# A graph layer and a mixture of experts in one kernel: the self-loop by VectorE, counts behind the last unit, and another order of the power, the routing and the fills

## The chip, the cores and the metric

The kernel runs on one core of a Trainium2 chip. The metric is the device time of the whole program in microseconds; lower is better. The engines are TensorE (PE), VectorE (DVE), ScalarE (ACT), GpSimd (POOL) and SyncE (SP), which only issues DMAs here.

## The reference

2048 tokens of 256 features and a 2048 x 2048 adjacency of zeros and ones:

```python
deg = jnp.maximum((adj != 0).astype(jnp.float32).sum(-1), 1.0)
# gnn: a_hat = adj + eye; a_norm = dinv * a_hat * dinv; pooled = a_norm @ x + x; relu(pooled @ W + b)
x = x + _L0_gnn_ref(_layernorm(x), adj, deg[..., None], W, b)
# ffn: gate, top 1 of 8 experts, softmax of one = 1; silu/gate/down per expert; plus gelu(xf @ sw1.T) @ sw2.T
x = x + _L0_ffn_ref(_layernorm(x)[None], gate_w, w1, w2, w3, sw1, sw2)[0]
```

(The kernel scales both sides by one inverse degree per row.) The eye in `a_hat` is the self-loop: each token's own row of z = norm(x) @ W is added to its neighbours' sum.

## The kernel before, in words

All matmuls are float32 split into a high half (fp32r) and a low half (the rest), and run as several fp32r products. For every operand some engine copies the high half (mostly ACT) and another subtracts it to get the low half (mostly POOL, with `tensor_tensor` from SBUF).

*Stages.* The first quarter computes z for 16 tiles of 128 tokens and adds up neighbours for output tiles 0 to 3. `agg_quarter(q)` for q = 1, 2, 3 does the same for four more output tiles each: 16 input tiles j, each with eight matmuls (L1304, L1306) that need `a_hi` (ACT, L667) and `a_lo` (POOL, L477) of that tile. Then `agg_end` (L1310 to L1315) adds the self-loop by four matmuls of `ident_r` with z. `gate` and `degrees` follow; `degrees` needs the neighbour counts of DVE (L922, L925). Then comes, for q = 1 and 2, a shared stretch of 16 units m (`shared`): `shared_up(m)` (L1405), gelu and `gel_hi` on ACT (L726, L730), `gel_lo` on POOL (L490), and two units later `shared_down` (L1427, L1429), which waits for `gel_lo`. Behind the fourth quarter the stretch has 32 units (LAST to LAST + 31), of which DVE makes the last `gel_lo`s (from LAST + DVE_AT on). In between, PE does gate, rank and transpose work for the routing. At last come 23 steps of expert work (`up`, `hid_transposes`, `down`), one for each block of 128 sorted rows.

*Order.* Every engine's order is written out by hand; semaphores tie them. Within the shared stretches POOL and ACT also make the first eight tiles' halves of the next quarter (`LEAD` = 8), one between two pairs of units. POOL makes `exp_of_z` (a power, L548) there behind the fourth of these. The other eight tiles' halves follow in the quarter itself, each when PE has freed its slot. The adjacency comes in chunks of two tiles in four buffers `araw`; the load of chunk n (L380) waits until chunk n - 4 is counted and split. POOL issues the `scatter` of sorted rows (L554): four behind the low halves of a quarter for an earlier quarter, and eight more among the last units.

*SP's order at the end.* It issues the expert chunks n = 0, 1, ... (L417; 12 an expert, four buffers), each waiting for the low half (`elo_ok`) of n - 3. Ahead of n = 8 it writes eight fill rows (L409), behind n = 11 it waits for all scatters, for the routing table (`routed`) and for the fills, and loads the first three blocks of sorted rows (L425), one behind each of n = 11, 12, 13. DVE makes the low halves of expert chunks 0 to 7 (`low_chunk`, L1155), POOL those from 8 on (L520).

*What the change touches on DVE.* `first_products` (L999) and `finish_gnn` (L1006, L1010) turn the neighbour sums into the new x, in the order `low * dinv2 + (z + bias)`, then `agg * dinv2 + low`, then relu and residual. `add_bias` (L916) makes z + bias in place. The loop from L1101 has the counts, statistics and `scales` of each quarter.

## Time and profile before

| | us |
|---|---|
| median of 3 runs (lowest, highest) | 475.96 (475.58, 478.83) |
| profiled execution, its own time | 476.37 |
| its span | 474.6 |
| PE busy | 445.6 (94%) |
| POOL busy | 322.6 (68%) |
| DVE busy | 255.2 (54%) |
| ACT busy | 208.4 (44%) |
| chain that ended last: PE, POOL, DVE, ACT | 72%, 11%, 6%, 4% |

All times below are from the start of the span. A row of a timeline has the start, the length, the engine (with q: its queue of instructions, mostly DMA issues), the line, what is written and read, the number of instructions merged, and in brackets the idle time before it and who ended that. An instruction that waits for a shared resource after its start is listed with that time in its length.

### The profile page before, as it was taken

Reading aid. Unit: us, or ns where it says so; the run is one execution under the profiler, and the core shown is the slowest. Engines: PE = TensorE matmul, PEld = TensorE weight load, DVE = VectorE, ACT = ScalarE, POOL = GpSimd, SP = SyncE. Lnnn points to the kernel's source line nnn. Section 1 sums busy time; section 2 is a strip of 40 time slices with the busy share of each in tenths; the row PEclk is TensorE's granted clock in tenths of the full one; section 3 lists DMA queues with packets and bytes.
Section 4 is the critical chain, followed back from the end, with each engine's and each line's share of the span. In section 5 each row is a group of like instructions: output and inputs, shape, how many; then the busy total and the mean of one; then the engine's idle time right before and its main releaser. Section 6 shows DMA issues by size and latency. Waiting matters only on the chain.

```text
span 474.6 us, 8852 instructions
## 1 busy us (share of the span) xinstructions
PE 445.6 (94%) x2635; PEld 381.7 (80%) x2636; DVE 255.2 (54%) x540; ACT 208.4 (44%) x462; POOL 322.6 (68%) x296
## 2 busy tenths in 40 slices
PE   7889999989999899999898999999999999999992
PEld 6779777878888788888787888888888888888872
DVE  5884979663767455888934433343334334433430
ACT  4777596655456354645442323232323222322330
POOL 3548975897488765779875498885677579883112
PEclk9999999999999899999999999999999999999997
DMA  8555534130440407685665999997898552663000
GB/s 272 205 176 182 159 107 136 55 110 24 134 135 1 134 2 254 228 310 207 195 200 151 377 353 378 339 341 240 305 330 303 184 203 36 75 79 44 2 0 0
DMA packets 39612, 82.61 MB, mean 174 GB/s; under 512 B 5024, under 2 KB 14752, under 8 KB 37536
## 3 DMA queue, kind: packets, MB, share of 16 engines
q1 hardware_dynamic: 27024, 47.60, 30.8%
q0 software_dynamic: 7536, 29.39, 20.2%
q10 hardware_dynamic: 5024, 5.27, 3.6%
q8 instruction: 15, 0.25, 0.2%
q14 instruction: 13, 0.11, 0.1%
HBM read 74.74 MB, written 8.41 MB: 175 GB/s over the span
## 4 chain that ended last, share of the span: by engine, by line
PE 72%; POOL 11%; DVE 6%; ACT 4%; issue 3%; DMA 2%; SPq 1%; POOLq 0%; ACTq 0%; DVEq 0%
PE bank L1486 26%; PE bank L1513 9%; PE bank L1304 9%; PE bank L1514 5%; PE bank L1306 4%; PE bank L1499 4%; POOL gel_lo L490 4%; PE bank L1405 4%; PE bank L1427 3%; PE bank L1262 2%; POOL a_lo L477 2%; POOL ering L520 2%; PE bank L1429 1%; PE bank L1288 1%; POOL sorted_x L554 1%
## 5 line engine op out<-in xcount | busy, mean ns | idle before, releaser
L1486 PE MATMUL bank<-ering,xsT_hi 128*128 x368 | 121.7, 402 | 1.4 <-POOL ering L520 1.4
L477 POOL TENSOR_TENSOR a_lo<-araw,a_hi 128x512 fp32r<-128x512 f32 x48 | 69.9, 1467 | 28.4 <-ACT a_hi L667 27.8
L1220 DVE SCALAR_TENSOR_TENSOR hid<-bank,xs,sil 128x512 f32<-128x512 f32 x46 | 34.5, 751 | 93.9 <-ACT sil L803 93.9
L1486 PEld LDWEIGHTS bank<-ering,xsT_hi 128*128 128x128 f32 x368 | 69.4, 189 | 17.8 <-issue 1.9
L1486 PE MATMUL bank<-ering,xsT_lo 128*128 x184 | 73.0, 396 | 0.0
L1304 PE MATMUL bank<-zz,a_hi 128*128 128x512 f32 x192 | 69.9, 404 | 2.4 <-POOL a_lo L477 2.4
L803 ACT ACTIVATE sil<-bank 128x512 f32<-128x512 f32 x46 | 27.5, 598 | 101.4 <-PE bank L1486 101.4
L520 POOL TENSOR_TENSOR ering<-eraw,ering 128x512 fp32r<-128x512 f32 x40 | 51.4, 1303 | 29.2 <-DMA ering<-in_experts 20.3
L1513 PE MATMUL bank<-ering,hidT_hi 128*128 x184 | 67.5, 407 | 1.2 <-DVE hidT_lo L1228 1.2
L520 POOL TENSOR_TENSOR ering<-eraw_more,ering 128x512 fp32r<-128x512 f32 x48 | 60.6, 1292 | 8.3 <-PE bank L1262 5.1
L625 POOL DMA_INDIRECT out<-y_rows,row_token x23 | 35.8, 1554 | 36.8 <-DVE y_rows L1236 31.4
L1427 PE MATMUL bank<-sw_r,gel_hi 128*128 128x512 f32 x128 | 50.4, 415 | 8.7 <-POOL gel_lo L490 6.9
L1306 PE MATMUL bank<-zz,a_lo 128*128 128x256 f32 x192 | 53.8, 280 | 0.0
L490 POOL TENSOR_TENSOR gel_lo<-gel,gel_hi 128x256 fp32r<-128x256 f32 x56 | 43.2, 778 | 14.9 <-ACT gel_hi L730 14.3
L1514 PE MATMUL bank<-ering,hidT_lo 128*128 x184 | 51.7, 281 | 0.0
L1304 PEld LDWEIGHTS bank<-zz,a_hi 128*128 128x128 f32 x192 | 36.1, 188 | 11.6 <-POOL a_lo L477 2.8
L1513 PEld LDWEIGHTS bank<-ering,hidT_hi 128*128 128x128 f32 x184 | 34.6, 188 | 8.7 <-issue 1.4
L925 DVE SCALAR_TENSOR_TENSOR count<-araw,count 128x1024 bf16<-128x1024 f32 x28 | 40.0, 1428 | 1.6
L1486 PEld LDWEIGHTS bank<-ering,xsT_lo 128*128 128x128 f32 x184 | 34.8, 189 | 7.3
L1405 PE MATMUL bank<-xfT_hi,sw_hi 128*128 128x256 f32 x128 | 37.3, 292 | 0.0
L1427 PEld LDWEIGHTS bank<-sw_r,gel_hi 128*128 128x128 f32 x128 | 24.7, 193 | 15.1 <-POOL gel_lo L490 6.7
L730 ACT ACTIVATE gel_hi<-gel 128x256 fp32r<-128x256 f32 x64 | 26.8, 418 | 22.5 <-PE bank L1429 22.2
(165 smaller groups left out, 931.1 us busy)
## 6 DMA issues: line engine op xcount, KB each, us to landing
araw<-in_adj_t SPq DMA_DIRECT2D x32, 512.0 KB, 4.5
eraw<-in_experts SPq DMA_DIRECT2D x48, 256.0 KB, 4.7
ering<-in_experts POOLq DMA_DIRECT2D x8, 1536.0 KB, 9.3
eraw_more<-in_experts SPq DMA_DIRECT2D x48, 256.0 KB, 5.9
ering<-in_experts POOLq DMA_DIRECT2D x8, 1024.0 KB, 7.1
ering<-in_experts POOLq DMA_DIRECT2D x8, 512.0 KB, 5.2
xs<-sorted_x ACTq DMA_DIRECT2D x20, 129.0 KB, 3.7
sw_raw<-in_sw_t ACTq DMA_DIRECT2D x2, 1024.0 KB, 7.5
```

Of the source, the lines that this page charges most:

```text
L477: pool.tensor_tensor(lo_part(s), araw[:, u // CJ, u % CJ, :], hi_part(s).bitcast(F32), ALU.subtract).then_inc(adj_lo_ok, 1)
L490: pool.tensor_tensor(gel_lo[:, u, :], gel[:, u, :], gel_hi[:, u, :].bitcast(F32), ALU.subtract).then_inc(sh_lo, 1)
L520: pool.tensor_tensor(ering[:, slot, 1, c * ECW:(c + 1) * ECW], raw, ering[:, slot, 0, c * ECW:(c + 1) * ECW].bitcast(F32), ALU.subtract).t ...
L625: pool.indirect_dma_start(out=out, out_offset=bass.IndirectOffsetOnAxis(ap=row_token[:, s:s + 1], axis=0), in_=y_rows[:, s, :], in_offset= ...
L925: dve.scalar_tensor_tensor(into, araw[:, r, :, :], 0.0, into, ALU.not_equal, ALU.add).then_inc(adj_counted, CJ)
L1304: pe.matmul(acc(q, it)[:, :], hi_part(s)[:, it * P:(it + 1) * P], zt, start=first, stop=False)
L1306: ins = pe.matmul(acc(q, it)[:, 0:D], lo_part(s)[:, it * P:(it + 1) * P], zt[:, 0:D], start=False, stop=False)
L1405: ins = pe.matmul(up_bank(m)[:, 0:HALF], w[:, k, ib * P:(ib + 1) * P], a[:, q % 2, k, half * HALF:(half + 1) * HALF], start=n == 0, stop=n ...
L1427: pe.matmul(shared_bank(hq, k)[:, :], gel_hi[:, m % 2, k * P:(k + 1) * P], sw2_r[:, ib, :, :].rearrange("p h d -> p (h d)"), start=ib == 0 ...
L1486: ins = pe.matmul(bank[2 * w + h][:, :], a[:, k, :], ering[:, bass.ds(slot, 1), part, at:at + BANK].rearrange("p a n -> p (a n)"), start=n ...
L1513: pe.matmul(bank[6][:, :], hidT_hi[:, k, :], w2, start=k == 0, stop=False)
L1514: ins = pe.matmul(bank[6][:, 0:D], hidT_lo[:, k, :], ering[:, bass.ds(slot, 1), 0, W2AT + k * D:W2AT + (k + 1) * D].rearrange("p a n -> p ...
```

## The change

- `agg_end` is left out in the second and third quarter (q = 1, 2; `by_vector`). DVE adds z itself: `first_products` adds `norm` (which stays z) to the low sums, `finish_gnn` adds the high ones, and one more pass multiplies by `dinv2` and adds z + bias from a new tile `z_bias`.
- DVE's counts of the next quarter's first three chunks wait for the stretch's last `gel_lo`.
- For q > 1 ACT takes the square root for the scales ahead of tile 8's high half, and the scaled rows behind tiles 9 and 10; DVE adds the bias behind the fourth count.
- POOL's power stands alone between two pairs; the low halves of the adjacency behind it move down by one pair, and the last two stand together.
- At the end: units LAST + 24 and 25 go to POOL; DVE adds shared sums 5 and makes `low_chunk` 4 to 7 ahead of the routing table; SP loads the first rows behind n = 13 instead of 11, and writes five of the eight fills ahead of n = 20; ACT waits for them ahead of its loop.

```diff
-    DVE_AT = 24
+    DVE_AT = 26
-    FIRST_AT, FIRST_ROWS = EC - 1, 3
+    FIRST_AT, FIRST_ROWS = EC + 1, 3
+    FILLS_AT = 2 * EC - ER
...
-                    if n == MORE:
+                    if n == MORE or n == FILLS_AT:
-                        for a in range(E):
+                        for a in range(FIRST_ROWS) if n == MORE else range(FIRST_ROWS, E):
...
-                        adj_lows(q + 1, j, j + 1)
-                        if j == AR - 1:
+                        if j < AR - 1:
+                            adj_lows(q + 1, j, j + 1)
+                        elif j == AR - 1:
                             exp_of_z(q - 1)
+                        else:
+                            adj_lows(q + 1, j - 1, j)
+                    adj_lows(q + 1, LEAD - 1, LEAD)
...
             scatter(3, 3, 4)
+            shared_lows(LAST + 24, 2)
...
+                if q > 1:
+                    stds(NQ + q - 1)
                 for j in range(ring(q), NT - 1 if q == 1 else NT):
...
+                    if by_vector(q):
+                        chained(dve.tensor_tensor(low, low, norm[:, t, :], ALU.add))
...
+                    if by_vector(q):
+                        chained(dve.tensor_tensor(low, agg[:, it, :], low, ALU.add))
...
+                if by_vector(q):
+                    for it in range(QT):
+                        low = acc(q, it)[:, D:2 * D]
+                        chained(dve.scalar_tensor_tensor(low, low, dinv2[:, it:it + 1], z_bias[:, it, :],
+                                                         ALU.mult, ALU.add))
+                    settle()
...
-                else:
-                    add_bias(q)
                 count_chunks(q, 3, RAW)
                 if q == 1:
                     shared_pieces(3, 5)
+                else:
+                    add_bias(q)
...
                     add_shared(2 * (q - 1))
+                    dve.wait_ge(sh_lo, q * 2 * NI)
                     count_chunks(q + 1, 0, 3)
...
+            add_shared(2 * NQ - 3)
+            for c in range(EARLY, MORE):
+                low_chunk(c)
             step(dve.tensor_tensor(r_s[:], per_e(ends[:], STEPS), s_iota[:], ALU.is_le))
...
-            for c in range(EARLY, MORE):
-                low_chunk(c)
-            add_shared(2 * NQ - 3)
...
-                agg_end(q)
+                if not by_vector(q):
+                    agg_end(q)
```

Three places in the instructions' order. First POOL in the first shared stretch, from the pair of units 6 and 7 on; `gel_lo` rows are pairs of units, `a_lo` rows the next quarter's tiles. Before:

```order
L490 TENSOR_TENSOR gel_lo<-gel,gel_hi 128x256 x2
L477 TENSOR_TENSOR a_lo<-araw,a_hi 128x512
L548 TENSOR_TENSOR weight<-e_base,weight 128x4
L490 TENSOR_TENSOR gel_lo<-gel,gel_hi 128x256 x2
L477 TENSOR_TENSOR a_lo_more<-araw,a_hi_more 128x512
```

and now:

```order
L496 TENSOR_TENSOR gel_lo<-gel,gel_hi 128x256 x2
L554 TENSOR_TENSOR weight<-e_base,weight 128x4
L496 TENSOR_TENSOR gel_lo<-gel,gel_hi 128x256 x2
L483 TENSOR_TENSOR a_lo<-araw,a_hi 128x512
L496 TENSOR_TENSOR gel_lo<-gel,gel_hi 128x256 x2
```

The power has the place between two pairs to itself, and tile 3's low half went down by one pair.

Then DVE from the end of the first shared stretch into the third quarter (`resid` rows are the shared sums, `rows<-rows,bias` the bias). Before:

```order
L922 TENSOR_SCALAR count<-araw 128x1024
L925 SCALAR_TENSOR_TENSOR count<-araw,count 128x1024 x2
L1042 TENSOR_TENSOR resid<-bank,resid 128x256 x2
L1049 TENSOR_TENSOR resid<-bank,resid 128x256 x2
L860 BN_STATS stats<-resid 128x6 x4
L865 BN_AGGR mv<-stats 128x2 x4
L886 RECIPROCAL rstd<-std 128x4
L888 SCALAR_TENSOR_TENSOR shift<-mv,rstd 128x4
L916 TENSOR_TENSOR rows<-rows,bias 128x256 x4
L925 SCALAR_TENSOR_TENSOR count<-araw,count 128x1024 x3
L1017 TENSOR_TENSOR xfT_lo<-bank,xfT_hi 128x2x2x128 x2
```

and now (the first row waits for the stretch's last gel_lo, which the order doesn't show):

```order
L940 TENSOR_SCALAR count<-araw 128x1024
L943 SCALAR_TENSOR_TENSOR count<-araw,count 128x1024 x2
L1073 TENSOR_TENSOR resid<-bank,resid 128x256 x2
L1080 TENSOR_TENSOR resid<-bank,resid 128x256 x2
L877 BN_STATS stats<-resid 128x6 x4
L882 BN_AGGR mv<-stats 128x2 x4
L903 RECIPROCAL rstd<-std 128x4
L905 SCALAR_TENSOR_TENSOR shift<-mv,rstd 128x4
L943 SCALAR_TENSOR_TENSOR count<-araw,count 128x1024
L934 TENSOR_TENSOR z_bias<-rows,bias 128x256 x4
L943 SCALAR_TENSOR_TENSOR count<-araw,count 128x1024 x2
L1048 TENSOR_TENSOR xfT_lo<-bank,xfT_hi 128x2x2x128 x2
```

The order is the same but for one count ahead of the bias; the first three counts, and all behind them, start later.

Last SP, from the expert loads behind the fill rows to the first sorted rows. Before:

```order
L409 DMA sorted_x<-pad_row 128x258
L417 DMA eraw<-in_experts 128x512 x4
L424 TENSOR_LOAD step_row
L424 ISA x2
L425 ISA
L425 DMA xs<-sorted_x 128x258
```

and now:

```order
L415 DMA sorted_x<-pad_row 128x258
L423 DMA eraw<-in_experts 128x512 x6
L430 TENSOR_LOAD step_row
L430 ISA x2
L431 ISA
L431 DMA xs<-sorted_x 128x258
```

Two more expert loads, each with its wait for a low half, stand ahead of the first rows.

## Rows read from the trace of the kernel before

**Rows 1.** Groups of instructions by line, from 80 to 110 us:

```profile
L1427 PE MATMUL bank<-sw_r,gel_hi 128*128 128x512 f32 x32 | 12.4, 410 | 3.0 <-POOL gel_lo L490 3.0
```

**Rows 2.** Busy time by stretch (engine busy, count; clock; DMA), both shared stretches:

```profile
81.30:109.27 27.97, 24.94 (x186) 22.10 (x182) 16.98 (x38) 16.71 (x41) 24.00 (x25) 1.00 0.31 97
134.47:163.24 28.77, 26.07 (x183) 23.14 (x181) 16.93 (x38) 16.72 (x41) 25.19 (x27) 0.94 0.28 91
```

**Rows 3.** Timeline of PE, first shared stretch, three waits for gel_lo:

```profile
84.11 0.48 PE L1427 MATMUL bank<-sw_r,gel_hi 128*128 128x512 f32 x1 [0.39 <-POOL gel_lo L490]
...
97.06 0.47 PE L1427 MATMUL bank<-sw_r,gel_hi 128*128 128x512 f32 x1 [0.46 <-POOL gel_lo L490]
...
104.69 0.50 PE L1427 MATMUL bank<-sw_r,gel_hi 128*128 128x512 f32 x1 [1.77 <-POOL gel_lo L490]
```

**Rows 4.** Timeline of POOL and DVE around 100 to 105 us, one instruction each:

```profile
100.25 1.58 DVE L925 SCALAR_TENSOR_TENSOR count<-araw,count 128x1024 bf16<-128x1024 f32 x1
...
100.69 2.28 POOL L477 TENSOR_TENSOR a_lo_more<-araw,a_hi_more 128x512 fp32r<-128x512 f32 x1
...
101.96 2.10 DVE L925 SCALAR_TENSOR_TENSOR count<-araw,count 128x1024 bf16<-128x1024 f32 x1
```

**Rows 5.** Busy time and granted clock of one microsecond, second stretch:

```profile
160.00:161.00 1.00, 1.00 (x5) 0.90 (x4) 0.00 (x0) 0.04 (x2) 0.39 (x1) 0.50 0.43 166
```

**Rows 6.** Timeline of PE and DVE, end of the second quarter:

```profile
79.23 1.10 PE L1313 MATMUL bank<-zz,ident_r 128*128 128x512 f32 x4
80.16 0.40 PE L1381 MATMUL bank<-xfT_hi,gate_r 128*16 128x512 f32 x1
...
81.11 0.35 PE L1322 MATMUL bank<-ones,count 128*128 128x1 bf16 x8
...
78.41 2.58 DVE L925 SCALAR_TENSOR_TENSOR count<-araw,count 128x1024 bf16<-128x1024 f32 x2
```

**Rows 7.** DVE's groups by shape, 135 to 141 us, and its timeline at 142:

```profile
L1006 DVE SCALAR_TENSOR_TENSOR bank<-agg,dinv,bank 128x256 f32<-128x256 f32 x4 | 1.7, 484 | 0.0
...
142.85 0.19 DVE L1034 COPY logit<-bank 128x32 f32<-128x32 f32 x1 [2.63 <-PE bank L1391]
```

**Rows 8.** Timeline of PE, DVE and POOL, the third quarter:

```profile
107.67 0.74 POOL L490 TENSOR_TENSOR gel_lo<-gel,gel_hi 128x256 fp32r<-128x256 f32 x1 [0.39 <-ACT gel_hi L730]
...
109.27 0.40 PE L1304 MATMUL bank<-zz,a_hi 128*128 128x512 f32 x1
...
126.71 0.48 PE L1304 MATMUL bank<-zz,a_hi_more 128*128 128x512 f32 x1
...
109.47 0.76 DVE L1042 TENSOR_TENSOR resid<-bank,resid 128x256 f32<-128x256 f32 x2 [5.42 <-PE bank L1429]
...
112.36 0.38 DVE L865 BATCH_NORM_AGGREGATE mv<-stats 128x2 f32<-128x6 f32 x4
...
127.32 2.54 POOL L477 TENSOR_TENSOR a_lo_more<-araw,a_hi_more 128x512 fp32r<-128x512 f32 x2 [6.31 <-ACT a_hi_more L667]
...
136.34 1.45 POOL L490 TENSOR_TENSOR gel_lo<-gel,gel_hi 128x256 fp32r<-128x256 f32 x2 [0.51 <-ACT gel_hi L730]
```

**Rows 9.** Timelines at the end of the shared stage; first, the chain's last scatter:

```profile
229.01 4.34 DMA sorted_x<-rows,pos
...
231.19 5.56 POOL L520 TENSOR_TENSOR ering<-eraw,ering 128x512 fp32r<-128x512 f32 x4 [0.92 <-DMA eraw<-in_experts]
...
232.87 0.47 PE L1427 MATMUL bank<-sw_r,gel_hi 128*128 128x512 f32 x1 [1.57 <-DVE gel_lo L1209]
...
234.12 0.34 SPq L425 DMA_DIRECT2D xs<-sorted_x  x1
...
239.30 0.38 PE L1262 MATMUL bank<-ident,xs 128*128 128x128 f32 x2
...
251.67 0.50 PE L1486 MATMUL bank<-ering,xsT_hi 128*128 x1 [1.38 <-POOL ering L520]
```

**Rows 10.** DMA issues of the page (KB each, us to landing):

```profile
xs<-sorted_x SPq DMA_DIRECT2D x3, 129.0 KB, 3.8
```

More of the change, by code:

```diff
@@ L171, in gnn_moe @@
     assert more_at[0] <= front[0]
+    z_bias = place("z_bias", [P, QT, D], F32, [front[0]])
     w_raw = place("w_raw", [P, KD, D], F32, front)
@@ L834, in _ @@
             hid_highs(0)
+            act.wait_ge(filled, 16 * (1 + E))
             with act.Fori(0, (STEPS - 3) // XR) as i:
@@ L1291, in z_tile, with agg_part @@
                 ins.then_inc(z_ps, 1)
-            def agg_part(q, j, s, n, first=False):
+            def agg_part(q, j, s, n, first=False, last=False):
                 pe.wait_ge(adj_lo_ok, n + 1)
```

39 lines of the change are left out of this document (24 added, 15 removed).

## The prediction, made before the changed kernel was run

> **What bounds the kernel now.** I read four views in this order: the waits, the busy time by stretch, the timelines around the places where the TensorE (PE) waits, and the DMA part of the page. PE is the bound: it waits little, and for nothing as long as for GpSimd (POOL) to finish gel_lo, the low half of a gelu: 3.0 us in the first of the shared stretches [rows 1]. A stretch of sixteen shared-expert units takes 27.97 us the first time and 28.77 us the second [rows 2]. So an edit is worth what it takes from PE's own work or from these waits, and no more.
>
> Two of the waits are the change's targets; a third, 0.39 us at 84.11 [rows 3], is the stretch's first gelu and stays. One of 0.46 us at 97.06 comes behind a POOL pair (a low half of the adjacency and the power `weight`). One of 1.77 us at 104.69 [rows 3] comes where VectorE (DVE) counts neighbours while POOL computes low halves. The reader is to see in [rows 4] how these two engines collide: the count that starts at 100.25 ends at 101.83; POOL's low half is listed from 100.69 to 102.97, which is 1.14 us behind the count's end, though such an operation takes 1.3 us from its own start (two take 2.54 [rows 8]); the next count, listed from 101.96, ends at 104.06, 1.09 us behind the low half. They go one after the other, never together, and the gel_lo in line behind them is late.
>
> **The change part by part.**
>
> *Self-loop by DVE.* PE loses four matmuls in the second and four in the third quarter. Four of them occupy it from 79.23 to the next operation at 80.16, so 0.93 us a quarter [rows 6]. In the second quarter this doesn't get through: the degrees at 81.11 need counts that end only at 78.41 + 2.58 = 80.99 [rows 6]; gain 0.1 us. In the third it does, but see the next part but one. DVE gets one pass more of four operations, 1.7 us, like the pass in [rows 7]. Its cover is the 2.63 us in which DVE waits for the gate's transposes [rows 7]; PE comes to them at most 0.9 us sooner, so 1.7 us fits by a hair. Without the cover it would cost up to 1.7 us a quarter.
>
> *The power's own pair, and counts behind the last unit.* In both shared stretches POOL never again has more than one operation between two pairs of gel_lo, and the counts run when the last gel_lo is done. The first stretch then loses all its waits but the first: 3.0 - 0.4 = 2.6 us [rows 1, 3]. The second has the same waits and is 28.77 - 27.97 = 0.8 us longer [rows 2]; right behind its long wait the granted clock was 0.50, the 1.2 GHz level, in the microsecond from 160 [rows 5]. With the wait gone I take that too: 2.6 + 0.8 = 3.4 us.
>
> *What the counts now collide with.* This is the price. In the third quarter (frame of before, PE's sixteen tiles start at 109.27) the last gel_lo ends at 107.67 + 0.74 = 108.4 [rows 8]. Three counts of 1.1 us alternate with the two low halves that POOL has left (1.14 each): 5.6 us at most, I take 5.4, so until 113.8. Then come the add of the shared sums and the statistics, which took from 109.47 to 112.74, 3.3 us [rows 8]: 117.1. ScalarE (ACT) now takes the square root in front of tile 8's high half, and four tiles of it (8 to 11) that POOL had done by then wait with it; tile 8's high half comes at 118.0. DVE has a count first in line, until 118.8. From there eight low halves (9.1 us), two counts (2.2) and four bias adds (a quarter of a count each, 1.2) share one port: the eighth low half ends at 131.3. Before, it ended at 127.32 + 2.54 = 129.86 [rows 8], because it waited for a DMA that now starts earlier. PE needs tile 8 at 109.27 + 8 x 1.39 = 120.4 (it comes at 120.0), and tile 14 at 126.71 + 2 x 1.39 = 129.5 [rows 8], where it comes at 130.1: a wait of 0.6, which eats into the 0.93 of the self-loop. Behind the low halves POOL issues four scatters before gel_lo of the next stretch, at 136.34 [rows 8]. They come 1.4 us later, gel_lo at 137.4, and nothing that PE saved before it counts any more: a net loss of 1.1 us. The fourth quarter repeats it; there the low halves ended later already, so 0.9 us. The ends: if the port costs nothing, the third quarter gains 0.9 and the fourth loses nothing; if each collision costs as drawn and tile 14 holds PE at the 1.2 GHz level afterwards, another 0.8 is lost in each.
>
> Here the Trainium skill, "SBUF — State Buffer", section "SBUF: two separate sides", bears on the row: VectorE with two SBUF inputs and a GpSimd operation that reads SBUF exclude each other for the whole instruction, whoever is first. By that rule, [rows 4] agree; it speaks against this change, since the counts are moved onto the low halves that feed PE. Taken for the scatters too (they read their row numbers from SBUF), it would put the last count behind a scatter of about 1 us and the degrees 0.6 us later in both quarters, a sum of some 473.5 in the place of mine.
>
> *The end of the shared stage.* POOL takes units 24 and 25 itself; DVE has added the shared sums and done its four expert lows before, ahead of the routing table. The 1.57 us in front of 232.87 [rows 9] go. But POOL begins its four expert lows 0.7 us later (231.19 to 231.9), and SP now issues two more expert loads ahead of the first sorted rows; the second of these waits for the second of the four lows, 5.56 / 4 = 1.4 us each [rows 9], so until 234.7. With its issue (0.4) and the reading of the row number (0.8: the last scatter landed at 229.01 + 4.34 = 233.35 and the rows were issued at 234.12) the first rows are issued at 235.9 and land 3.8 us later [rows 9, 10], at 239.7. PE would be ready at 239.30 - 1.57 = 237.7 and waits 2.0 us: against 239.30 [rows 9] a loss of 0.4 us. With the fastest landing that I would grant, 2.9 us, it is a gain of 0.5. Five of the eight fills go behind n = 19, which gives SP time where the four expert loads waited, and takes it ahead of loads that only the second step's down part needs, more than 10 us later: nothing.
>
> *The sum* against the profiled execution's own 476.37 us: -0.1 - 2.6 + 1.1 - 3.4 + 0.9 + 0.4 = -3.7, which is 472.7. The median of the runs is 475.96, 0.09% lower; so I expect a median of 472.3.
>
> **The rivals.**
> (a) *The port is shared better, or the rows land early.* For it: POOL has idle time before 127.32, and DVE's bias adds are short. Against it: [rows 4]. The third and fourth quarters give back 2.9 us; with 0.5 instead of -0.4 at the end it is 468.5.
> (b) *PE's clock falls at the new waits.* The two new waits of about 2 us (before the next stretch's first down part, and for the first rows) (1.7 and 2.0 us) are as long as the one behind which it fell, the second stretch's twin of 104.69 [rows 3, 5]. For it: that row; against it: the same wait at 104.69 left it up. 0.8 us each, and 0.9 where the wait meets the expert's matmuls at once: 474.0.
> (c) *The low halves come late in earnest: slower.* If a count or add stands between any two low halves, at 1.14 + 1.09 = 2.23 us each, the eighth ends at 118.8 + 17.8 = 136.6. PE needs it at 130.9 and the scatters follow: the loss is 136.6 - 129.9 less the 0.3 us that gel_lo had to spare, 6.4 us instead of 1.1 in the third quarter, and 6.2 instead of 0.9 in the fourth: 472.3 + 10.6 = 482.9. It turns the sign where the eighth ends behind 133.1, 1.85 us more lost in each. Against it: DVE has only seven such operations there, four of them short.
> (d) *The removed waits come back.* If POOL, at 2 x 0.74 + 1.29 = 2.8 us a pair against PE's 2.8, has no slack whatever DVE does, the waits shrink by half only: 472.3 + 3.0 = 475.3. Against it: units 0 to 5 run so without any wait of PE.
> (e) *The last wait.* 1.38 us before 251.67 [rows 9] are put down to expert lows. If that is so, earlier loads take it away, 470.9; but PE also reads two registers there, which would leave it.
>
> **How the numbers follow.** Forecast 0.40, (a) 0.22, (b) 0.16, (c) 0.06, (d) 0.06, (e) 0.10. The forecast's own range is 470.8 to 473.8. The range for 8 in 10 is 468.4 to 475.0, which leaves out (c), most of (d) and a little below (a). About 1%, 4.8 us, is what a measurement of this kernel can tell from no change: faster by over 1% (under 471.2) are (a), half of (e) and a fifth of the forecast, 0.35; slower by over 1% is (c) and what I haven't seen, 0.07; within 1% the rest, 0.58.
>
> **What would show it.** In the changed profile: the first shared stretch at 25.4 us and no gel_lo wait over 0.5 us in it (right) or waits left behind a low half (d). The counts start behind the stretch's last gel_lo, and the high half of tile 8 about 8.7 us behind PE's first tile. The eighth low half at 22 us behind it (forecast), under 20.5 (a), over 24 (c). The first gel_lo of the next stretch right behind the fourth scatter, with PE waiting about 2 us. The first sorted rows issued about 4 us behind POOL's first expert low, PE waiting for them. The granted clock in both places decides (b). My prediction is wrong in its core if the first stretch keeps its length, or if DVE's longer finish holds up the gate's transposes.

## The result and the profile after

| | before | after |
|---|---|---|
| median (lowest, highest), us | 477.22 (475.51, 481.15), 20 runs | 474.98 (472.89, 476.45), 20 runs |
| profiled span, us | 474.6 | 473.3 |
| PE, POOL, DVE, ACT busy, us | 445.6, 322.6, 255.2, 208.4 | 444.7, 328.4, 267.3, 207.5 |

The ratio is 0.9944, with a 95% interval of 0.9927 to 0.996: the changed kernel is faster by 0.6%, which is under the 1% named in the prediction. The median lies 2.7 us above the forecast of 472.3 and at the upper edge of its range, inside it by 0.02 us, which is less than the 0.2 us between two series of the same kernel (474.98 here, 474.75 in e11): that it fell inside is luck. The kernel before had a median of 475.96 in its first three runs and of 477.22 in twenty, so 1.3 us of these 2.7 are its own spread.

PE's waits in the profile after (engine, what it was to write, line, releaser: us in total, times, longest):

```profile
PE bank L1460 <- POOL gel_lo L496: 4.6, 8, 1.6
...
PE bank L1294 <- DMA xs<-sorted_x: 1.4, 1, 1.4
```

The rows of its timeline that answer to those of before. First PE, in the order of time: the last gel_lo wait of the first stretch, PE's first tile of the third quarter, tile 14, the next stretch's first down part, the last gel_lo wait of the second stretch, tile 15 and the first down part of the fourth quarter:

```profile
105.10 0.50 PE L1460 MATMUL bank<-sw_r,gel_hi 128*128 128x512 f32 x1 [0.51 <-POOL gel_lo L496]
...
106.78 0.40 PE L1336 MATMUL bank<-zz,a_hi 128*128 128x512 f32 x1
...
127.82 0.50 PE L1336 MATMUL bank<-zz,a_hi_more 128*128 128x512 f32 x1 [0.54 <-POOL a_lo_more L483]
...
135.88 0.48 PE L1460 MATMUL bank<-sw_r,gel_hi 128*128 128x512 f32 x1 [1.64 <-POOL gel_lo L496]
...
156.70 0.49 PE L1460 MATMUL bank<-sw_r,gel_hi 128*128 128x512 f32 x1 [0.51 <-POOL gel_lo L496]
...
181.74 0.50 PE L1336 MATMUL bank<-zz,a_hi_more 128*128 128x512 f32 x1 [0.66 <-POOL a_lo_more L483]
...
188.38 0.47 PE L1460 MATMUL bank<-sw_r,gel_hi 128*128 128x512 f32 x1 [0.52 <-POOL gel_lo L496]
```

The waits of 0.46 and 1.77 us in [rows 3] are gone. Behind tile 14 the longest wait is now the 1.64 us for the next stretch's first gel_lo. To see where the time went I divided every profile at the same kinds of row: the first `shared_up` of a stretch, its first `shared_down`, and the first aggregation matmul of the quarter behind it; then the first transpose of sorted rows and the first matmul of the second and third expert step. (From the first `shared_up` to the first `shared_down` it is 2.78 us in both.)

| stretch of PE's time, us | before | after | difference | forecast |
|---|---|---|---|---|
| start to first shared_up | 81.32 | 81.53 | +0.2 | -0.1 |
| first shared_down to third quarter | 25.16 | 22.47 | -2.7 | -2.6 |
| third quarter to its first shared_down | 27.95 | 29.10 | +1.15 | +1.1 |
| first shared_down to fourth quarter | 26.02 | 22.49 | -3.5 | -3.4 |
| fourth quarter to its first shared_down | 28.03 | 30.00 | +2.0 | +0.9 |
| 32-unit stretch to the first sorted rows | 48.04 | 47.87 | -0.2 | +0.4 |
| to the second step (L1519) | 12.37 | 12.59 | +0.2 | 0 |
| second to third step | 9.55 | 10.95 | +1.4 | 0 |
| third step to the end | 213.42 | 213.55 | +0.1 | 0 |

Five of the first six rows came within 0.6 us of the forecast. Two rows missed it by over a microsecond: the fourth quarter by 1.1 us and the second expert step by 1.4 us. The experiments below look at both.

The second expert step is a matter of the granted clock. Busy times of PE, PEld, DVE, ACT and POOL in the 3 us behind its start, with the granted clock (the seventh number is PEclk):

```profile
249.00:252.00 3.00, 3.00 (x8) 2.32 (x9) 1.19 (x4) 0.00 (x0) 1.98 (x2) 0.50 0.80 295
```

0.50 is the 1.2 GHz level. It lasted 3.4 us, from 248.7, behind PE's gaps of 0.59 and 1.43 us at the end of the first step.

### The profile page after: what moved, and what is told of

It is laid out like the page before. It is cut to its first block, busy times and chain, and to the rows that moved or that the text cites. A ratio compares the mean times of both kernels' runs of the same rounds, so it can differ in the third digit from the quotient of the medians.

```text
span 473.3 us, 8845 instructions
## 1 busy us (share of the span) xinstructions
PE 444.7 (94%) x2627; PEld 380.1 (80%) x2628; DVE 267.3 (56%) x546; ACT 207.5 (44%) x462; POOL 328.4 (69%) x298
## 4 chain that ended last, share of the span: by engine, by line
PE 63%; POOL 12%; DVE 12%; issue 7%; ACT 4%; DMA 1%; POOLq 0%; SPq 0%; DVEq 0%; ACTq 0%
PE bank L1519 28%; PE bank L1546 9%; PE bank L1547 5%; PE bank L1532 4%; PE bank L1438 4%; POOL a_lo_more L483 3%; POOL a_lo L483 3%; DVE count L943 3%; PE bank L1460 3%; POOL sorted_x L560 2%; PE bank L1336 2%; POOL gel_lo L496 2%; PE bank L1294 2%; DVE stats L877 2%; PE bank L1320 1%
## 5 line engine op out<-in xcount | busy, mean ns | idle before, releaser
L1519 PE MATMUL bank<-ering,xsT_hi 128*128 x368 | 122.8, 405 | 1.5 <-issue 1.4
L483 POOL TENSOR_TENSOR a_lo<-araw,a_hi 128x512 fp32r<-128x512 f32 x48 | 72.4, 1525 | 37.1 <-ACT a_hi L678 37.1
L1519 PEld LDWEIGHTS bank<-ering,xsT_hi 128*128 128x128 f32 x368 | 70.0, 190 | 18.6 <-issue 2.5
L1519 PE MATMUL bank<-ering,xsT_lo 128*128 x184 | 73.4, 399 | 0.0
L1460 PE MATMUL bank<-sw_r,gel_hi 128*128 128x512 f32 x128 | 49.0, 405 | 4.6 <-POOL gel_lo L496 4.6
L943 DVE SCALAR_TENSOR_TENSOR count<-araw,count 128x1024 bf16<-128x1024 f32 x28 | 44.7, 1596 | 1.3
L1519 PEld LDWEIGHTS bank<-ering,xsT_lo 128*128 128x128 f32 x184 | 35.1, 191 | 7.5
L1338 PEld LDWEIGHTS bank<-zz,a_lo 128*128 128x128 f32 x192 | 36.3, 189 | 0.0
L1462 PE MATMUL bank<-sw_r,gel_lo 128*128 128x256 f32 x128 | 35.9, 280 | 0.0
```

Of the source, the lines that this page charges most:

```text
L483: pool.tensor_tensor(lo_part(s), araw[:, u // CJ, u % CJ, :], hi_part(s).bitcast(F32), ALU.subtract).then_inc(adj_lo_ok, 1)
L943: dve.scalar_tensor_tensor(into, araw[:, r, :, :], 0.0, into, ALU.not_equal, ALU.add).then_inc(adj_counted, CJ)
L1338: ins = pe.matmul(acc(q, it)[:, 0:D], lo_part(s)[:, it * P:(it + 1) * P], zt[:, 0:D], start=False, stop=last)
L1460: pe.matmul(shared_bank(hq, k)[:, :], gel_hi[:, m % 2, k * P:(k + 1) * P], sw2_r[:, ib, :, :].rearrange("p h d -> p (h d)"), start=ib == 0 ...
L1462: ins = pe.matmul(shared_bank(hq, k)[:, 0:D], gel_lo[:, m % 2, k * P:(k + 1) * P], sw2_r[:, ib, 0, :], start=False, stop=ib == NI - 1)
L1519: ins = pe.matmul(bank[2 * w + h][:, :], a[:, k, :], ering[:, bass.ds(slot, 1), part, at:at + BANK].rearrange("p a n -> p (a n)"), start=n ...
```

## The experiments

### The self-loop: e3_end_back and e10_root10_end_back

The first is the changed kernel with the self-loop back on PE; the second undoes it in the kernel of e5 below.

```diff
         def by_vector(q):
-            return 0 < q < NQ - 1
+            return False
```

(The waits of POOL and ACT on `agg_sum` go back with it.)

> The changed kernel, with the self-loop of the second and third quarter back on TensorE (four matmuls of 0.93 us a quarter), VectorE's finish short again; all else as changed. Theory of the prediction: in both quarters the four matmuls lie beside waits that hold PE anyway (the degrees' counts in the second; the fourth scatter and the first gel_lo in the third), so the total changes by 0 to +0.3 us. Rival (PE's work counts in full): +0.9 us in the third quarter and +0.9 in the second, total +1.8 us. Second rival (DVE's longer finish is what makes the third quarter's low halves late): total -1 us.

> The kernel with the square root ahead of tile 10's high half, and with the self-loop of the second and third quarter back on TensorE. In the changed kernel putting it back cost 0.10 us in the second quarter (held by the counts) and 0.00 in the third (held by the low halves and scatters). With the root at tile 10 nothing holds PE at the end of the third quarter any more. Theory: the four matmuls now count there in full, the third quarter to its first down wait is 0.9 us longer (28.2 instead of 27.32 us), the second 0.1 us, total +1.0 us. Rival (the degrees, the shared units' gelu or DVE hold PE there just as well): under 0.3 us.

In e3 the second quarter is 0.10 us longer (first shared_up at 81.63 for 81.53): PE has no wait there, where in the changed kernel it waits for the counts in front of the degrees:

```profile
81.32 0.35 PE L1354 MATMUL bank<-ones,count 128*128 128x1 bf16 x8 [0.73 <-DVE count L943]
```

The third quarter to its first shared_down takes 29.10 us in both kernels. The four matmuls of e3 and the wait behind them:

```profile
130.89 1.10 PE L1345 MATMUL bank<-zz,ident_r 128*128 128x512 f32 x4
...
136.01 0.47 PE L1460 MATMUL bank<-sw_r,gel_hi 128*128 128x512 f32 x1 [0.65 <-POOL gel_lo L496]
```

The matmuls are back and the wait for gel_lo is 0.65 instead of 1.64 us: PE's saving in the third quarter had become waiting. In the two quarters the theory held. In e10, where that wait is only 0.39 us (ACT's first gelu), the same four matmuls cost 28.26 - 27.32 = 0.94 us. So the self-loop is worth 0.1 us in the changed kernel and about 1 us where nothing else holds the quarter. For e10 the medians agree (472.16 beside 470.86 for e12, measured together). For e3 they don't: 476.02 is 1.0 us above the changed kernel, though its ratio, 0.9975 [0.9945, 1.0006], overlaps that kernel's. Four of its ten executions have a mean granted clock of 0.988 or less and none of the changed kernel's 28, which may be part of it; and in its profile PE waits 1.91 us for the first sorted rows instead of 1.40. Whether the self-loop has a part in either is open.

### The two shared stretches: e2_counts_early and e7_power_back

```diff
                     add_shared(2 * (q - 1))
-                    dve.wait_ge(sh_lo, q * 2 * NI)
                     count_chunks(q + 1, 0, 3)
```

> The changed kernel, with VectorE's counts no longer waiting for the stretch's last gel_lo (its wait taken out, they start when the shared sums are added, as in the kernel before). Theory (counts collide with GpSimd's last gel_lo): a gel_lo wait of 1.5 to 2 us comes back near the end of the first and of the second shared stretch, each of them is 1.5 to 2.5 us longer (from 25.3 to about 27 us), and the third and fourth quarter lose their give-back of 1.15 and 1.97 us at least by half, since DVE is through with the counts 4 us sooner: total +1 us (0 to +2.5). Rival (the power's own pair alone removed the waits): the stretches keep their 25 us and the quarters win, total -2 to -3 us.

PE's waits of the first stretch in e2:

```profile
99.82 0.50 PE L1459 MATMUL bank<-sw_r,gel_hi 128*128 128x512 f32 x1 [0.27 <-POOL gel_lo L496]
...
104.40 0.50 PE L1459 MATMUL bank<-sw_r,gel_hi 128*128 128x512 f32 x1 [1.23 <-POOL gel_lo L496]
...
107.03 0.50 PE L1459 MATMUL bank<-sw_r,gel_hi 128*128 128x512 f32 x1 [0.27 <-POOL gel_lo L496]
```

Both stretches grew by 2.2 us (24.69 and 24.71 for 22.47 and 22.49), and the two quarters shrank by 1.67 and 1.65 us (27.43 and 28.35). So the late counts win 4.4 us in the stretches and give 3.3 back in the quarters: a net gain of 1.1 us. (Against the mean of six profiles, 59.5 us for both quarters, which the section on the tie explains, they give 3.7 back, and 0.8 is left.) The medians of the two kernels (475.09 and 474.98) can't tell such a difference.

e7 puts the power back behind a low half in the same gap:

```diff
-                        if j < AR - 1:
-                            adj_lows(q + 1, j, j + 1)
-                        elif j == AR - 1:
+                        adj_lows(q + 1, j, j + 1)
+                        if j == AR - 1:
                             exp_of_z(q - 1)
-                        else:
-                            adj_lows(q + 1, j - 1, j)
-                    adj_lows(q + 1, LEAD - 1, LEAD)
```

> The changed kernel, with GpSimd's power back in its place behind a low half of the adjacency in the same gap between two pairs of gel_lo, all low halves behind it one pair sooner. Theory: only the short wait of about 0.46 us in the middle of each shared stretch comes back, 0.3 to 0.6 us per stretch, total +0.5 to +1.1 us (third to fourth quarter unchanged); the counts' wait is then the one that was worth some 2 us a stretch. Rival (POOL has no slack in the stretch, and the two are not independent): over 1 us per stretch. Second rival (the power was hidden anyway, the last low half now standing alone costs as much): 0.

PE's longer waits in the first stretch of e7, behind its first down part:

```profile
97.27 0.47 PE L1456 MATMUL bank<-sw_r,gel_hi 128*128 128x512 f32 x1 [0.46 <-POOL gel_lo L496]
...
105.75 0.50 PE L1456 MATMUL bank<-sw_r,gel_hi 128*128 128x512 f32 x1 [0.44 <-POOL gel_lo L496]
```

The wait of 0.46 us is back where it was in [rows 3], at 97. The first stretch took 23.17 us, 0.7 more than in the changed kernel and a little over the 0.3 to 0.6 expected. (The second took 24.74, but with a stretch at half clock in it, from 137.0 on, so it says little.) So in the first stretch, undoing the power alone costs 0.7 us and undoing the counts alone 2.2. Together that is 2.9 for the 2.7 gained, so the two hardly depend on each other.

### The square root's place: e1_root_back, e5_root_at_10 and e12_root10_again

In the third and fourth quarter the changed kernel has ACT's square root (`stds`) ahead of tile 8's high half. In the kernel before it stood behind tile 11's. e1 puts it back there; e5 puts it ahead of tile 10's; e12 is e5 once more.

```diff
-                if q > 1:
-                    stds(NQ + q - 1)
                 for j in range(ring(q), NT - 1 if q == 1 else NT):
+                    if q > 1 and j == LEAD + 2:
+                        stds(NQ + q - 1)
                     adj_highs(q, j, j + 1)
```

(This is e5. Its scaled rows go behind tiles 10 and 11.)

> The changed kernel, with ScalarE's square root and scaled rows of the third and fourth quarter put back to their place in the kernel before (square root behind the high half of tile 11). Theory (the root in front of tile 8's high half holds GpSimd's low halves): GpSimd's idle time of 6.6 us ahead of tile 8's low half in the third quarter shrinks by over half, the eighth low half ends at 20.5 us behind PE's first tile or sooner, and what the third quarter (first aggregation matmul to the end of the first down wait: +1.15 us against the kernel before) and the fourth (+1.97 us) give back shrinks together to under 1.0 us: 2 to 3 us less in all, about 472.5 where the changed kernel has 475. Rival (the late counts on the shared port do it, wherever the root stands): the statistics come no earlier, the low halves go on alternating with counts and bias adds, and the two quarters keep at least 2.5 of the 3.1 us. Second rival: PE's waits move to the degrees or to the gate's transposes, since the scaled rows are late.

> The changed kernel, with ScalarE's square root of the third and fourth quarter ahead of tile 10's high half instead of tile 8's (scaled rows behind tiles 10 and 11). Its high halves of tiles 8 and 9 need nothing that the statistics need, so GpSimd can do two low halves (2.6 us) while VectorE is still in the statistics, and the reciprocal still comes at 8.3 us behind PE's first tile as in the changed kernel. Theory (the root in front of tile 8 wastes GpSimd's time, the counts behind it must not be late either): the eighth low half ends at 20.0 to 21.5 us behind PE's first tile (22.2 in the changed kernel, 22.5 with the root behind tile 11), the wait for tile 14 goes, and the third and fourth quarter to the end of the first down wait take 28.0 to 28.5 us each (29.1 and 30.0 in the changed kernel): 2 to 2.5 us less in all. Rival (with the port full from then on, the last two low halves wait for their own chunk and meet the counts wherever the root stands): third quarter within 0.5 us of 29.1.

> The kernel with the square root ahead of tile 10's high half once more, in five rounds beside the changed kernel. Theory: the third and fourth quarter take 27.3 and 28.5 us again, and the median lies 3.3 us below the changed kernel's, at about 471.5 us (469.8 in its first runs). Rival (the first runs only had fewer disturbed stretches): under 1.5 us below.

| | changed kernel | e1 | e5 | e12 |
|---|---|---|---|---|
| root stands | ahead of tile 8 | behind tile 11 | ahead of tile 10 | ahead of tile 10 |
| third quarter to its first shared_down, us | 29.10 | 29.33 | 27.32 | 27.11 |
| fourth, us | 30.00 | 28.46 | 28.46 | 28.36 |
| median of its runs, us | 474.98 | 473.48 | 469.78 | 470.86 |

In the changed kernel POOL and DVE in the third quarter (PE's first tile is at 106.78; the rows are POOL's low halves, and DVE's reciprocal, fourth count, bias adds and the four other counts with the transposes' low halves between them):

```profile
115.42 2.13 POOL L483 TENSOR_TENSOR a_lo<-araw,a_hi 128x512 fp32r<-128x512 f32 x1 [6.55 <-ACT a_hi L678]
...
121.84 7.17 POOL L483 TENSOR_TENSOR a_lo_more<-araw,a_hi_more 128x512 fp32r<-128x512 f32 x4
...
114.85 0.18 DVE L903 RECIPROCAL rstd<-std 128x4 f32<-128x4 f32 x1 [0.36 <-ACT std L652]
...
115.17 1.23 DVE L943 SCALAR_TENSOR_TENSOR count<-araw,count 128x1024 bf16<-128x1024 f32 x1
116.32 5.85 DVE L934 TENSOR_TENSOR z_bias<-rows,bias 128x256 f32<-128x256 f32 x4
122.08 4.54 DVE L943 SCALAR_TENSOR_TENSOR count<-araw,count 128x1024 bf16<-128x1024 f32 x2
126.55 1.28 DVE L1048 TENSOR_TENSOR xfT_lo<-bank,xfT_hi 128x512 fp32r<-128x512 f32 x2
127.75 3.71 DVE L943 SCALAR_TENSOR_TENSOR count<-araw,count 128x1024 bf16<-128x1024 f32 x2
```

POOL stands idle for 6.55 us, and then each of its low halves meets an operation of DVE: the bias adds take 1.46 us each instead of 0.42, two counts 4.54 (in e1, undisturbed, 2.57). In e1 (PE's first tile is at 108.30):

```profile
114.08 2.55 POOL L483 TENSOR_TENSOR a_lo<-araw,a_hi 128x512 fp32r<-128x512 f32 x2 [3.69 <-ACT a_hi L678]
117.56 2.54 POOL L483 TENSOR_TENSOR a_lo<-araw,a_hi 128x512 fp32r<-128x512 f32 x2 [0.93 <-ACT a_hi L678]
120.21 3.62 POOL L483 TENSOR_TENSOR a_lo_more<-araw,a_hi_more 128x512 fp32r<-128x512 f32 x2
126.09 4.67 POOL L483 TENSOR_TENSOR a_lo_more<-araw,a_hi_more 128x512 fp32r<-128x512 f32 x2 [2.26 <-ACT a_hi_more L678]
...
119.65 0.18 DVE L901 RECIPROCAL rstd<-std 128x4 f32<-128x4 f32 x1 [3.64 <-ACT std L652]
...
120.04 1.21 DVE L941 SCALAR_TENSOR_TENSOR count<-araw,count 128x1024 bf16<-128x1024 f32 x1
...
121.47 5.05 SPq L386 DMA_DIRECT2D araw<-in_adj_t  x2
```

Four low halves are done early and undisturbed (1.27 us each), but DVE waits 3.64 us for the root, and its fourth count comes at 120.04. The load of the quarter's last chunk into the same buffer goes out only behind it (121.47; in the changed kernel at 116.61), so POOL waits 2.26 us more and its last two low halves meet two counts, 2.3 us each. Its eighth low half ends 22.5 us behind PE's first tile, where 20.5 was expected. In the third quarter the theory was wrong: one delay took the place of the other. The fourth takes 1.5 us less, but 1.1 of these are the tie of the next section, which the changed kernel's first profile had lost there: against the 28.94 us of e11 they are 0.5. In e5 (PE's first tile is at 106.45) both are avoided:

```profile
112.10 2.54 POOL L483 TENSOR_TENSOR a_lo<-araw,a_hi 128x512 fp32r<-128x512 f32 x2 [3.56 <-ACT a_hi L678]
115.36 3.30 POOL L483 TENSOR_TENSOR a_lo<-araw,a_hi 128x512 fp32r<-128x512 f32 x2 [0.72 <-ACT a_hi L678]
118.61 6.58 POOL L483 TENSOR_TENSOR a_lo_more<-araw,a_hi_more 128x512 fp32r<-128x512 f32 x4
125.38 1.97 POOL L560 DMA_INDIRECT sorted_x<-rows,pos  x1 [0.19 <-issue]
...
114.52 0.18 DVE L903 RECIPROCAL rstd<-std 128x4 f32<-128x4 f32 x1 [0.36 <-ACT std L652]
...
133.77 0.47 PE L1460 MATMUL bank<-sw_r,gel_hi 128*128 128x512 f32 x1 [0.39 <-POOL gel_lo L496]
```

Two low halves run while DVE is still in the statistics, the reciprocal waits 0.36 us as in the changed kernel, and the eighth low half ends at 125.19, 18.7 us behind PE's first tile (22.2 in the changed kernel; I had expected 20.0 to 21.5). The wait for tile 14 is gone, and that for the first gel_lo is down to the 0.39 us of the gelu. This place is the fastest of the three: 469.78 us in four executions and 470.86 in six more, with ratios to the kernel before of 0.9849 [0.9785, 0.9913] and 0.9848 [0.9813, 0.9883]. The changed kernel, measured again beside the second series, had 474.75 us and 0.9921 [0.9892, 0.995]: 3.9 us more, for 3.3 expected.

### A tie at the last low half: e11_after_again and e8_count_after_low

> The changed kernel once more, unchanged. If the place of the 3.4 us stretch at half clock (248.7 us in the changed kernel's profile, 137 and 13.5 us in others, none in some) and the winner of the tie between a count and the last low half vary by execution, this profile differs from the first in at least one of them by 1 to 1.5 us, with every other stretch equal within 0.1 us; if they belong to the program, it repeats them both: 29.1 and 30.0 us for the third and fourth quarter to their first down waits, and 10.95 us for the second expert step.

In the changed kernel POOL's eighth low half and DVE's next to last count are issued within 0.02 us of each other. The first profile, third and then fourth quarter:

```profile
127.73 1.28 POOL L483 TENSOR_TENSOR a_lo_more<-araw,a_hi_more 128x512 fp32r<-128x512 f32 x1
127.75 2.35 DVE L943 SCALAR_TENSOR_TENSOR count<-araw,count 128x1024 bf16<-128x1024 f32 x1
...
179.34 2.35 POOL L483 TENSOR_TENSOR a_lo_more<-araw,a_hi_more 128x512 fp32r<-128x512 f32 x1
```

In the third POOL goes first and the count waits; in the fourth the low half waits for the count. POOL's last low halves in the fourth quarter of the first profile, and then of e11, the third and the fourth quarter (three low halves each):

```profile
173.44 8.25 POOL L483 TENSOR_TENSOR a_lo_more<-araw,a_hi_more 128x512 fp32r<-128x512 f32 x4
```

```profile
124.86 6.82 POOL L483 TENSOR_TENSOR a_lo_more<-araw,a_hi_more 128x512 fp32r<-128x512 f32 x3
...
177.56 5.73 POOL L483 TENSOR_TENSOR a_lo_more<-araw,a_hi_more 128x512 fp32r<-128x512 f32 x3
```

Where the count goes first, the same low halves take 1.08 us longer: 8.25 for 7.17 us in the first profile (fourth and third quarter), 6.82 for 5.73 in e11 (third and fourth). The first profile has it in the fourth quarter, e11 in the third: 29.10 and 30.00 us in the one, 30.18 and 28.94 in the other, with the same instructions. e3, e4, e6 and e13 leave these two quarters' low halves and counts as they are in the changed kernel. In these six profiles POOL went first in the third quarter in three and in the fourth in one. POOL's is listed as the earlier in all twelve cases, by 6 to 19 ns: it won at 13, 14, 14 and 19 ns and lost at 6 to 10, but also at 15 and 17. Apart from the tie and a half-clock stretch (at 13.7 us in e11, 248.7 in the first profile), the two profiles of the changed kernel agree within 0.4 us in every stretch of the table, where 0.1 had been expected.

```diff
+                if q > 1:
+                    dve.wait_ge(adj_lo_ok, (q + 1) * NT)
                 count_chunks(q, NC - 2, NC)
```

> The changed kernel, with one wait more: VectorE's second but last count of the third and fourth quarter waits for the quarter's last low half. In the changed kernel both are issued within 0.02 us of each other; GpSimd's went first in the third quarter (low half done at 22.2 us behind PE's first tile) and the count in the fourth (23.3). Theory (this tie decides 1.08 us): the fourth quarter to its first down wait takes 28.9 to 29.1 us instead of 30.0, the third stays at 29.1 or below, total -1.0 us. Rival (the count then comes late for the degrees): the wait for the degrees grows by 1 us and nothing is gained.

POOL in the fourth quarter and DVE in the third of e8:

```profile
175.20 7.36 POOL L483 TENSOR_TENSOR a_lo_more<-araw,a_hi_more 128x512 fp32r<-128x512 f32 x4
...
130.68 2.58 DVE L943 SCALAR_TENSOR_TENSOR count<-araw,count 128x1024 bf16<-128x1024 f32 x2 [1.28 <-issue]
```

The four low halves of the fourth quarter take 7.36 instead of 8.25 us. The quarters take 29.33 and 29.32 us: the fourth 0.68 less than in the first profile, not the 1.0 expected, and the third 0.23 more. Against a mean of 59.5 us for both quarters over the six profiles, the wait is worth 0.8 us (its median, 474.12, is 0.9 below the changed kernel's).

### The first sorted rows: e4_rows_at_11 and e6_rows_at_12

```diff
-    FIRST_AT, FIRST_ROWS = EC + 1, 3
+    FIRST_AT, FIRST_ROWS = EC - 1, 3
```

(This is e4. e6 has `EC`.)

> The changed kernel, with SyncE issuing the first sorted rows behind expert chunk 11, as in the kernel before, in place of chunk 13. Theory: PE's wait of 1.40 us for the first sorted rows goes, the rows being issued about 2 us earlier, and PE comes to its second step 1.4 us earlier (247.4), total -1.4 us if nothing is late behind it; the half clock that followed at 248.7 may go too (another -1.4). Rival (SyncE then issues chunks 12 and 13 of the expert loads later and something in step 1 or 2 waits for them, or the rows wait for the scatters anyway): under 0.5 us.

> The changed kernel, with the first sorted rows issued behind expert chunk 12 (in the changed kernel 13). With 11, PE began its first expert step 0.5 to 0.9 us sooner, but waited 0.9 and 1.5 us for low halves of expert chunks in the third and fifth step. Theory (the loads of the rows push back the expert loads behind them, one load's worth for each place): with 12 the wait for the rows is 0 to 0.7 us, the later waits together 0.5 to 1.2 us, total within 0.7 us of the changed kernel. Rival (the later waits come from something else and vary by execution): no wait over 0.5 us for an expert chunk, total -1 us.

PE in e4, the third and the fifth step, then the fifth in e6, and the fifth in e12, whose first rows stand where the changed kernel has them:

```profile
278.53 0.50 PE L1519 MATMUL bank<-ering,xsT_hi 128*128 x1 [0.86 <-POOL ering L526]
...
299.45 0.49 PE L1519 MATMUL bank<-ering,xsT_hi 128*128 x1 [1.48 <-POOL ering L526]
```

```profile
299.27 0.49 PE L1519 MATMUL bank<-ering,xsT_hi 128*128 x1 [0.83 <-POOL ering L526]
```

```profile
295.24 0.49 PE L1519 MATMUL bank<-ering,xsT_hi 128*128 x1 [1.02 <-POOL ering L526]
```

| us | changed kernel | e6, behind 12 | e4, behind 11 |
|---|---|---|---|
| 32-unit stretch to the first sorted rows | 47.87 | 46.31 | 46.11 |
| to the second step | 12.59 | 13.08 | 13.47 |
| third step to the end | 213.55 | 214.39 | 216.30 |

The wait for the rows goes in both, but 0.5 and 0.9 us of it come back at once. The sum of the three rows is 0.2 us lower in e6 and 1.9 us higher in e4. A wait in the fifth step proves nothing about the place of the rows: e2, e7 and e12, which have them behind 13, wait there for 0.76, 0.35 and 1.02 us, and e5, with the same instructions as e12, not at all. So the 0.83 us of e6 fits its rival (the later waits vary by execution) as well as its theory. In e4 the wait in the third step, 0.86 us, stands in no other profile, and 1.48 is the longest in the fifth; there the expectation's rival, that later loads make a later wait, is likely but rests on one profile. Which load is late was not followed further.

### The last gel_lo's and the expert low halves: e13_units_back

```diff
-    DVE_AT = 26
+    DVE_AT = 24
...
-            shared_lows(LAST + 24, 2)
...
-            add_shared(2 * NQ - 3)
-            for c in range(EARLY, MORE):
-                low_chunk(c)
             step(dve.tensor_tensor(r_s[:], per_e(ends[:], STEPS), s_iota[:], ALU.is_le))
```

(The two calls go back behind the routing table, and DVE's first and second sums one unit down.)

> The changed kernel, with the end of the shared stage as before in one part: GpSimd makes gel_lo only up to unit LAST + 23, VectorE the last eight, and VectorE makes its four expert low halves and adds shared sums 5 behind the routing table; the first rows stay behind chunk 13. Theory (the prediction's): the wait of about 1.6 us for VectorE's gel_lo of unit LAST + 24 comes back, and the wait for the first rows (1.40 us) shrinks by as much, since the rows are issued at the same time or 0.7 us earlier: from the start of the 32-unit stretch's down parts to the first step nothing changes by more than 0.5 us. Rival (the removed wait was worth its full 1.57 us): the same distance grows by 1.2 to 1.6 us.

Both expectations failed: 480.33 us, ratio 1.0039 [1.0005, 1.0072], slower than the kernel before. POOL, DVE and PE at the place:

```profile
228.09 7.37 POOL L526 TENSOR_TENSOR ering<-eraw,ering 128x512 fp32r<-128x512 f32 x6
...
229.19 6.90 DVE L1240 TENSOR_TENSOR gel_lo<-gel,gel_hi 128x256 fp32r<-128x256 f32 x2
...
235.89 0.77 PE L1459 MATMUL bank<-sw_r,gel_hi 128*128 128x512 f32 x1 [6.79 <-DVE gel_lo L1240]
```

DVE issued unit LAST + 24's gel_lo at 229.19, while POOL was in the first of six expert low halves, and didn't get it done before POOL had finished the sixth at 235.46. PE waited 6.79 us, and during the wait its clock fell to the lower level (for 6.8 us, from 232.0). In the kernel before, the same operation met the same low halves and came second, behind one of them: there the wait is 1.57 us [rows 9]. DVE's row of before:

```profile
231.38 2.77 DVE L1209 TENSOR_TENSOR gel_lo<-gel,gel_hi 128x256 fp32r<-128x256 f32 x2
```

The nearest to it elsewhere is one expert low half of DVE in each profile that let two gel_lo's pass (2.34 to 2.36 us); no other operation of DVE here was passed by more than one of POOL's. What made POOL keep the port five times in a row here is open; both operations and their forms are the same as in the kernel before. The loss is not one execution's: the median of ten is 5.4 us above the changed kernel's, the profile 6.3 (its wait and the half clock, less the wait for the first rows, which is gone). The run puts three things back at once, the units, the expert low halves and the sums; which of them brings the two operations together was not taken apart.

## Why the prediction was right or wrong, point by point

*The second quarter's self-loop, -0.1.* Right: putting it back cost 0.10 us (e3). The profile of after is 0.2 us longer up to there than that of before, but e5 and e12, with the same instructions up to that point, have 81.16 and 81.20 us for its 81.53, so 0.1 or 0.2 us is within the spread of executions. That the 0.93 us bought nothing is shown by the 0.73 us wait that took their place.

*The first shared stretch, -2.6.* Right, in size (-2.7) and in cause: undoing the counts costs 2.2 us (e2), undoing the power 0.7 (e7). A wait that the forecast had at nothing, 0.51 us at 105.10, stays.

*The third quarter, +1.1.* Right in the total and in its working. The first low half of the quarter started 8.64 us behind PE's first tile (forecast: tile 8's high half at 8.7), the eighth ended at 22.24 (22.0), tile 14 waited 0.54 us (0.6), and PE waited 1.64 us for the first gel_lo behind the fourth scatter (1.7). That PE's 0.93 us would buy nothing there is what e3 shows, and e10 shows that it was this wait that swallowed it.

*The second stretch, -3.4.* The waits' part, 2.6, is right: the stretch is 3.5 us shorter, of which 0.86 is what it had over the first one. The 0.8 us of clock came as forecast, but one profile was too little to take it from. Of fourteen profiles four show no half-clock stretch ahead of the program's tail; in the others such stretches, nearly all 3.4 us long, lie at 13.5, 137, 159, 232, 244 or 249 us. The changed kernel has one at 248.7 in its first profile, one at 13.7 in e11. Where they fall goes by the execution as much as by the program, and each costs 0.9 to 1.6 us. In the first profile of the changed kernel such a loss stands in the second expert step, +1.4.

On average the credit was due all the same. The mean granted clock is on record for every execution of the experiments: of 80 of the kernel before, 32 are at 0.988 or less, of 28 of the changed kernel none, and the means are 0.989 and 0.9925 (0.9887 and 0.992 where e11 and the kernel before were measured side by side). A 3.4 us stretch at half clock takes 0.0036 off the mean of an execution, so by this estimate the kernel before has about one such stretch more. At equal clock, 0.989 to 0.991, the medians are 476.92 us (35 executions) and 475.62 (13): 1.3 us apart, where all executions together are 2.5 apart. About half of the gain is then clock. Which edit brings it is not shown.

*The fourth quarter, +0.9.* This is the step that failed, a term too small, and it is hidden in the third quarter too: the forecast lets two counts stand between the low halves, and there can be three. It took it that the eighth low half and the next to last count share the port with POOL first. With POOL first, the third quarter gives back 1.15 us and the fourth 0.91 (e11), the forecast's 1.1 and 0.9. But it is a tie within 0.02 us, each tie lost costs 1.08 us, and in six profiles of this order it was lost in eight of twelve cases: 1.4 us a run that the sum did not have.

*The end of the shared stage, +0.4.* The working was right: PE was ready 46.47 us behind the stretch's first shared_down (forecast 239.30 - 1.57 - 191.27 = 46.46), and the first rows were issued 3.99 us behind POOL's first expert low half (about 4). The landing was mis-sized:

```profile
233.10 0.34 SPq L431 DMA_DIRECT2D xs<-sorted_x  x1
...
236.25 0.33 PE L1294 MATMUL bank<-ident,xs 128*128 128x128 f32 x1 [1.40 <-DMA xs<-sorted_x]
```

3.15 us instead of the 3.8 of [rows 10], so the wait is 1.40 us instead of 2.0, and the term is -0.2. That too is one execution: in the other profile of the same kernel the wait is 1.00 us. What the forecast didn't see is the price of leaving this part out: 6.8 us instead of 1.57 (e13). What this part holds off in the new order is far more than the wait that it removed in the old one.

*The rivals.* (a) Not in the changed kernel, but e5 and e12 are this rival made real by moving the square root with its scaled rows: the third quarter gains 0.6 to 0.8 us on the kernel before, the fourth loses 0.3 to 0.4, at 469.8 to 470.9 us. (b) The clock did fall in the first profile, but not at the two waits named, and in e11 it did not fall there at all. (c) Did not happen: the adds cost POOL 0.2 us a low half, and only two or three counts stood between low halves. (d) Refuted by e2 and e7, each of which brings back its own part. (e) Refuted: the releaser of that wait now reads

```profile
248.84 0.79 PE L1519 MATMUL bank<-ering,xsT_hi 128*128 x1 [1.43 <-issue]
```

and it is 1.34 to 1.77 us in every kernel here, those with earlier and with later expert loads. What PE's queue does in it (it reads the step's two registers there) was not taken away in a run.

*The rule on the shared port.* In the changed kernel a scatter that meets a count takes 1.97 us, one that meets none 0.96:

```profile
129.20 1.97 POOL L560 DMA_INDIRECT sorted_x<-rows,pos  x1 [0.19 <-issue]
...
134.02 0.96 POOL L560 DMA_INDIRECT sorted_x<-rows,pos  x1 [0.30 <-issue]
```

It starts at 129.20, the count that was running ended at 130.10, and the scatter took until 131.17; the last count, issued at 130.23 inside it, took its usual 1.23 us. So the scatter waited for the count, but the count did not wait for the scatter. The Trainium skill, "SBUF — State Buffer", section "SBUF: two separate sides", has a VectorE operation with two SBUF inputs and a GpSimd operation that reads SBUF exclude each other, whichever starts first. Taken for the scatter, as the prediction did, these rows agree with one direction and not with the other, and the sum of 473.5 rested on the other.

## What to carry to other kernels

- An instruction that waits for another engine's statistics should stand behind all the work in its queue that is ready before them, and ahead of the first work that waits for a slot: here two tiles decided 3.3 us (1.1 of it a lost tie), since too early a place idled one engine and too late a place delayed a load that hung on the next engine's release of a buffer.
- Where two engines share a port, look for operations that are issued at the same instant: a sum that takes one winner is wrong by a whole operation as often as the other wins. And the wait that a part of a change removes in the old order (1.57 us) can be a small part of what it holds off in the new one (6.8 us).
- Don't take a clock loss from one profile, for or against a change; compare the mean granted clocks of many executions. Here one profile made it look as if the loss had only moved, while over many executions about one stretch in each is gone.

## What the runs showed of the hardware

- Of two operations of DVE and POOL that start within 0.02 us and need the same port, either may go first, in two executions of the same program: 1.08 us here.
- Waiting for the port is not always one operation long: in e13 one DVE 128x256 subtraction was passed by five POOL operations of 1.25 us in a row and took 6.56 us.
- PE's granted clock fell to 1.2 GHz for 3.4 us at places that differ between executions of one program, at a cost of 0.9 to 1.6 us each. How often it fell differed between programs: the mean granted clock was 0.988 or less in 32 of 80 executions of the kernel before and in none of 28 of the changed one.
